# Gate and up products for two steps at once in 64x32 tiles, with fewer PSUM banks for outputs and features

## The reference

```python
x = x + _layernorm(attn(_layernorm(x), Wq, Wk, Wv, Wo))
# feed-forward, 512 -> 2048 -> 512, weights from cubic interpolation of control points
gate = einsum('bsh,ih->bsi', layernorm(x), gate_w)
up = einsum('bsh,ih->bsi', layernorm(x), up_w)
inter = silu(gate) * up
x = x + _layernorm(einsum('bsi,hi->bsh', inter, down_w))
```

## Time and profile before

| | us |
|---|---|
| median of 3 runs | 821.23 (818.14 to 821.86) |
| profiled execution | 818.13 |
| its span | 816.3 |
| first gate matmul of the feed-forward block | 413.4 |
| PE busy in the span | 742.2 (91%) |
| DVE, ACT, POOL busy | 530.1, 370.3, 445.9 |

### The profile page before, as it was taken

One profiled execution on the slowest core, in us unless ns is written; L12 is line 12 of the kernel. 1 busy time (PEld: TensorE's weight loads), 2 busy tenths in 40 slices (PEclk: granted clock), 3 DMA queues, 4 the chain that ended last, 5 costly groups with the idle time before them and its releaser, 6 DMA issues. The chain is left out here.

```text
span 816.3 us, 19133 instructions
## 1 busy us (share of the span) xinstructions
PE 742.2 (91%) x7152; PEld 506.3 (62%) x7152; DVE 530.1 (65%) x1025; ACT 370.3 (45%) x633; POOL 445.9 (55%) x616
## 2 busy tenths in 40 slices
PE   5887799999999999799857899999989999999996
PEld 3665577877687768677533466566656556565565
DVE  6752964587546863465656677878777787775453
ACT  2420332333232323232346666666656665666541
POOL 5289948556763759601425455455455555456542
PEclk9897799999999999989989999999999999999999
DMA  8614647333661448501881515545353553535313
GB/s 286 218 52 123 200 148 242 98 116 123 200 195 35 158 154 269 137 3 48 257 298 36 193 46 184 157 150 175 120 180 106 168 170 130 169 100 185 119 53 104
DMA packets 64313, 120.54 MB, mean 148 GB/s; under 512 B 12144, under 2 KB 28656, under 8 KB 62192
## 3 DMA queue, kind: packets, MB, share of 16 engines
q1 hardware_dynamic: 64240, 119.53, 45.2%
HBM read 82.94 MB, written 36.57 MB: 146 GB/s over the span
## 5 line engine op out<-in xcount | busy, mean ns | idle before, releaser
L1240 POOL TENSOR_TENSOR act<-inter,act 128x512 f16<-128x512 f32 x128 | 158.4, 1248 | 126.8 <-ACT act L1281 126.8
L1354 DVE SCALAR_TENSOR_TENSOR inter<-ubank,c_up,gated 128x512 f32<-128x512 f32 x128 | 95.9, 749 | 74.9 <-ACT gated L1285 74.2
L1494 PE MATMUL ybank<-down,act 128*128 128x160 f16 x512 | 110.5, 235 | 0.0
L1495 PE MATMUL ybank<-down,act 128*128 128x160 f16 x512 | 109.5, 233 | 0.0
L1496 PE MATMUL ybank<-down,act 128*128 128x160 f16 x512 | 109.5, 233 | 0.0
L1285 ACT ACTIVATE gated<-gbank,c_gate 128x512 f32<-128x512 f32 x128 | 87.9, 686 | 44.6 <-PE gbank L1453 44.6
L1281 ACT CAST act<-inter 128x512 f16<-128x512 f32 x128 | 79.1, 618 | 48.6 <-DVE inter L1354 48.5
L1494 PEld LDWEIGHTS ybank<-down,act 128*128 128x128 f16 x512 | 50.1, 98 | 39.2 <-issue 35.5
L1453 PE MATMUL gbank<-z,s_twice 128*32 128x512 f16 x512 | 51.8, 394 | 9.0 <-PEq L84 3.5
L728 PE MATMUL ybank<-ga_hi,xT_hi 128*128 128x512 f32 x128 | 51.8, 405 | 6.1 <-ACT shared L520 4.7
L520 ACT ACTIVATE shared<-ybank,yr 128x512 f32<-128x512 f32 x32 | 22.0, 689 | 71.9 <-POOL yr L363 71.9
(11 more groups left out here) (191 smaller groups left out, 2078.5 us busy)
## 6 DMA issues: line engine op xcount, KB each, us to landing
x_ln<-x SPq DMA_DIRECT2D x64, 256.0 KB, 3.3
z<-token_features SPq DMA_DIRECT2D x16, 1024.0 KB, 5.5
job<-job_in SPq DMA_DIRECT2D x24, 640.0 KB, 4.4
shared<-x SPq DMA_DIRECT2D x32, 256.0 KB, 2.7
x<-shared SPq DMA_DIRECT2D x32, 256.0 KB, 2.0
token_features<-z_hi SPq DMA_DIRECT2D x64, 128.0 KB
token_features<-z_lo SPq DMA_DIRECT2D x64, 128.0 KB
x_res<-x SPq DMA_DIRECT2D x32, 256.0 KB, 2.9
```

Of the source, the lines that this page charges most:

```text
L1240: pool.tensor_tensor(hidden[par][:, i, TOK:2 * TOK], inter[:, i % INTERS, :], hidden[par][:, i, 0:TOK], ALU.subtract).then_inc(inter_ready, 1)
L1354: dve.scalar_tensor_tensor(out=inter[:, i % INTERS, :], in0=ubank[:], scalar=c_up[:], in1=gated[:, i % 2, :], op0=ALU.mult, op1=ALU.mult). ...
L1494: pe.matmul(out, hidden[par][:, r, high], box[:, 0], start=False, stop=False)
L1495: pe.matmul(out, hidden[par][:, r, high], box[:, 1], start=False, stop=False)
```

## The change

**Gate and up.** `gate_up` is called once for two steps, i and i + 1. Its matmuls use 64 of the 128 rows and 32 columns, so that eight tiles fill the array: four column tiles times two row halves. For z, the two row halves now hold different tiles of the token features, with high and low values in different rows of the buffer (`u // 2 * 2 + low`). The products are high times high, high times low, low times high: three passes of eight matmuls for gate and three for up, for two steps, where there were eight passes of four. A step's eight halves go so that the two row halves of one column tile write to banks of different steps. Four banks hold gate and up of the two steps. A `sem_inc` on PE carries the wait for the banks.

**Banks.** The output banks become one (`outbank`), emptied by ACT for even q and by DVE for odd q; the last group uses gate and up banks beside it. The feature banks become one (`zbank`): `products` runs its half 0 in the second half of a quad and its half 1 in the first half of the next quad, after DVE has emptied half 0 (`z_half_ready`); the transpose of the next tile waits until half 1 is emptied.

**Order.** ACT, DVE and POOL do silu, product and rounding for pairs of steps. `load_z` is two DMAs of 64 partitions. The DRAM tensor has high and low beside each other.

```diff
-                    pe.wait_ge(z_loaded[par][i // HALF], count * 16)
-                side, c = i // HALF, i % HALF
-                for w, bank, free, done in ((GATE, gbank, silu_done, gate_done), (UP, ubank, inter_done, up_done)):
-                    if not (isinstance(n, int) and n == 0):
+                    pe.wait_ge(z_loaded[par][i // HALF], count * 32)
+                side, first = i // HALF, isinstance(n, int) and n == 0
+                for w, banks, free, done in ((GATE, gbanks, silu_done, gate_done), (UP, ubanks, inter_done, up_done)):
+                    if not first:
                         pe.wait_ge(free, n)
-                    for part, start in ((s_twice, True), (s_low, False)):
+                        pe.sem_inc(banks_free, 1)
+                    for part, low, start, stop in ((s_twice, 0, True, False), (s_twice, 1, False, False),
+                                                   (s_low, 0, False, True)):
                         for u in range(4):
-                            rows = slice(32 * u, 32 * u + 32)
-                            mm = pe.matmul(bank[rows], part[:, side, c, w, rows], z[par][:, i // 4 * 4 + u, :],
-                                           start=start, stop=not start)
-                    mm.then_inc(done, 1)
+                            for e in range(2):
+                                rows, at = slice(64 * (u % 2), 64 * (u % 2) + 64), 32 * (u ^ e)
+                                mm = pe.matmul(banks[e][at:at + 32],
+                                               part[rows, side, (i + e) % HALF, w, 32 * u:32 * u + 32],
+                                               z[par][rows, i // 4 * 4 + u // 2 * 2 + low, :], start=start, stop=stop)
+                    mm.then_inc(done, 2)
...
-        gbank, ubank, tbank, zbank = [psum(n, [P, BANK], F32) for n in ("gbank", "ubank", "turned", "zbank")]
-        ybank = [psum(f"ybank{q}", [P, BANK], F32) for q in range(2)]
+        gbanks = [psum(f"gbank{e}", [P, BANK], F32) for e in range(2)]
+        ubanks = [psum(f"ubank{e}", [P, BANK], F32) for e in range(2)]
+        zbank, ybank = [psum(n, [P, BANK], F32) for n in ("zbank", "outbank")]
...
-            def quad(g, par, count, j, made, begun, more):
+            def quad(g, par, count, j, made, begun, more, owed):
                 m = g * Q + j + AHEAD
                 first = isinstance(g, int) and g == 0
-                for s in range(4):
-                    i = 4 * j + s
+                for i in (4 * j, 4 * j + 2):
                     n = g * I + i
                     if i + 2 < I:
                         gate_up(n + 2, i + 2, par, count)
                     elif not (isinstance(n, int) and n >= STEPS - 2):
-                        gate_up(n + 2, i + 2 - I, 1 - par, count + par)
+                        gate_up(n + 2, 0, 1 - par, count + par)
+                    if i == 4 * j and owed:
+                        feats.products(pe, m - 1, z_banks, (1,))
                     if i == 0 and not first:
                         moment_pair(g - 1, I // 2 - 1, 1 - par)
-                    elif i % 2 == 0 and i:
+                    elif i:
                         moment_pair(g, i // 2 - 1, par)
                     if not first:
                         part(g - 1, i, 1 - par)
-                    if s == 1 and made:
+                    if i == 4 * j + 2 and made:
+                        feats.products(pe, m, z_banks, (0,))
+                    if not first:
+                        part(g - 1, i + 1, 1 - par)
+                    if i == 4 * j and made:
                         feats.turn(pe, m, z_banks, id16)
-                    if s == 2 and made:
-                        feats.products(pe, m, z_banks)
...
         sp.wait_ge(feats.z_spilled[half], (g + 1) * feats.SPILLS // 2 * 16)
-        sp.dma_start(z[:, half * self.half:(half + 1) * self.half, :],
-                     feats.spilled[half].rearrange("a k f t n -> (a k f) t n")).then_inc(self.z_loaded[par][half], 16)
+        pairs = self.half // 2
+        for two in range(2):
+            sp.dma_start(z[64 * two:64 * two + 64, half * self.half:(half + 1) * self.half, :],
+                         feats.spilled[half][:, :, two * pairs:(two + 1) * pairs].rearrange("k f t a n -> (k f) (t a) n")
+                         ).then_inc(self.z_loaded[par][half], 16)
```

More of the change, by code:

```diff
@@ L977, in turn_copy, with z_low @@
         dve.tensor_copy(self.hT[:].rearrange("p a k n -> p (a k n)"), banks[1].bitcast(F16)).then_inc(self.hT_copied, 1)
-    def z_low(self, dve, m, q, banks, buf=0):
+    def z_low(self, dve, m, q, banks, buf=0, halves=(0, 1)):
         K = self.K
         high, low_t = self.z_parts[buf]
-        for half in range(2):
+        for half in halves:
             dve.wait_ge(self.z_hi_done, m * 2 + half + 1)
@@ L1000, in turn, with products @@
         mm.then_inc(self.hT_done, 1)
-    def products(self, pe, m, banks):
+    def products(self, pe, m, banks, halves=(0, 1)):
         feat, hT = self.feat, self.hT
-        pe.wait_ge(self.hT_copied, m + 1)
-        for half in range(2):
+        for half in halves:
+            if half == 0:
+                pe.wait_ge(self.hT_copied, m + 1)
+            elif halves == (1,):
+                pe.wait_ge(self.z_half_ready, m + 1)
             cols = slice(half * self.ZCOLS, (half + 1) * self.ZCOLS)
@@ L1268, in _ @@
             low(0, 0, 0)
+            low(1, 1, 0)
             feats.scale(pool, Q + 2)
@@ new lines, in product_pair, with quad @@
+            def product_pair(g, i):
+                for e in range(2):
+                    product(g * I + (i + 2 + e), i + 2 + e)
+            def quad(g, par, count, j, made, begun, more, owed):
+                i, m = 4 * j, g * Q + j + AHEAD
+                loads = g + (1 + (j + AHEAD + 1) // RING)
+                for before, q in outputs(g, i, 0):
+                    if q % 2 == 1:
+                        y_out(before, q)
+                if made:
+                    feats.norm(dve, m, (j + AHEAD) % RING)
+                product_pair(g, i)
+                if owed:
+                    feats.z_low(dve, m - 1, (j + 1) % Q, z_banks, 1 - par if j == 3 else par, (1,))
+                if made:
+                    feats.low(dve, m)
+                if begun:
+                    feats.stats(dve, m + 1, (j + AHEAD + 1) % RING, loads)
+                for before, q in outputs(g, i, 0):
+                    o_stats(before, q)
+                if i == 0 and not (isinstance(g, int) and g == 0):
+                    moment_lo(g - 1, 1)
+                if made:
+                    feats.turn_copy(dve, m, z_banks)
+                if not (isinstance(g, int) and g == GROUPS - 1 and j == Q - 1):
+                    product_pair(g, i + 2)
+                if made:
+                    feats.z_low(dve, m, (j + 2) % Q, z_banks, par if j < 2 else 1 - par, (0,))
+                for before, q in outputs(g, i + 2, 2):
+                    o_finish(before, q)
+                if j == Q - 1:
+                    moment_lo(g, 0)
@@ L1766, in feature_tables @@
     assert (high.astype(np.float64) + low == feat).all()
-    features = np.stack([high, low], 1).reshape(P, 2, K, T * FEATURES)
+    halves = [t.reshape(P, K, 2, T // 4, 2, FEATURES).swapaxes(3, 4) for t in (high, low)]
+    features = np.stack(halves, 1).reshape(P, 2, K, T * FEATURES)
     return features, points.reshape(K * FEATURES, 5, -1), coef.reshape(K * FEATURES, 5, -1).astype(np.float32)
```

176 lines of the change are left out of this document (85 added, 91 removed).

## The result

The changed kernel takes **852.09 us** (median of 4 runs, 847.2 to 854.26), the one before 821.55 beside it (4 runs, 818.14 to 825.64): a ratio of 1.035, with an interval of 1.030 to 1.040. The change is slower by 3.5%. The forecast of 823 us and its range of 808 to 840 are both missed. "Slower" was the direction with the highest chance, 0.42. Of that, 0.20 was the upper part of case A, at most 831 us; the rest was put at 834 and at 857, each for a reason that isn't the one found.

A forecast was written before the change was run, and what follows sets the result against it. PE was taken as the bound, with the z refill next to no slack behind it; group terms summed to +1.2 us, with 0.3 us waits +2: 820 profiled, 823 us as median, range 808 to 840.

The forecast's parts named there:

- case A: The forecast itself: the z refill sets each group's length, three quarters of PE's gain turns idle; 815 to 831 us, chance 0.60.
- 857: Rival in gate/up: the two row halves take turns, 24 passes for 12, a group 53.5 us; 857 us, chance 0.10.
- PE's work: PE's quads: eight tiles run in the time of four, 0.96 us less a quad, 30.7 us less over 32 quads.
- The refill becomes the bound: Each group's first gate: PE idles some 4.3 us for the z load; the way around takes 47.4 us.
- The second z load: Refill on SP: z load as two DMAs adds a second issue of 0.34 us, 0.3 more; landing kept at 5.4.
- The clock: PE around first gates: idle time lowers the clock, costing 1.3 us a group, between 0 and 1.7.
- The loop's return: Groups 2 to 5: the stall of 2.1 us at 608 us stays, some 2.5 with its clock.
- Groups 1 and 6: From each one's first gate to the next group's: +0.4 us for group 1, +1.4 for group 6, before waits of 0.3 each.
- Group 0: First group: pairs make the chain of silu and products faster, then the refill's fixed 14 us follow; -1.0 us.
- Rival E: DVE: `o_finish` at a quad's end delays `h_lo` more than laid out, 1.5 us more a group; 834 us, chance 0.12.
- The start of the block: Stretch up to group 0's first gate: the sum has no term for it.
- Behind group 7's gate: After group 7's first gate, no refill: 3.5 quads gain 3.7 us, the clock gives back 1.3; -2.4 us.

The follow-up runs named there:

- b_twoload: Kernel before the change, with each half of z loaded by two DMAs of 64 partitions instead of one of 128: 837.42 us.
- a_warm: Changed kernel, with 22 matmuls whose sums nobody reads ahead of each wait for z, to keep PE busy: 844.83 us.
- a_early2: Changed kernel, SP spilling and loading z earlier, the output's store ahead of the z load, q = 0's high part waiting only for its own half's spill: 808.31 us.
- e2_norm: `a_early2` with DVE's norm of the next token block moved ahead of `z_low` of half 0: 804.45 us.
- b_norefill: Kernel before the change, without the refill of z (features spilled and loaded once, for group 0): 818.66 us.
- before: The kernel without the change: 821.55 us.
- after: The kernel with the change as made: 852.09 us.
- a_early: Changed kernel, SP spilling half 0 in quad 1 and loading it at once, ahead of the output's store; half 1 spilled at quad 2's start: 828.38 us.

## Why the prediction was wrong

By its own steps, for the profiled execution (820 forecast, 854.3 measured):

- **PE's work: right.** Eight tiles make a pass of 0.22 us, and a full group without refill gains 4.3 us against 3.8. PE's busy sum falls by the forecast 31 us between the kernels without refill; with it by only 14 (742 to 728), as matmuls at half clock count for longer.
- **The refill becomes the bound: right**, as the mechanism of case A, which had 0.60. The way around is also as laid out up to the spill: from the first gate to `o_finish` 29.2 to 30.3 us against 28.7 (in groups 2, 3, 5 and 6; the loop's return is in group 4), and from there to the first spill 3.7 to 7.5, in the mean 5.5 as forecast.
- **The second z load: mis-sized.** The sum gives it the 0.34 us of a second issue, which is SP's cost, and leaves the landing at 5.4. Measured are 7.1 to the last landing. From first spill to gate there are 16.4 to 16.8 us for the 14.8 of the sum, so 1.6 to 2.0 more in each of groups 1 to 6; with 1.3 in group 0 that is some 12 us. In the kernel before the same split costs 15.5 us in all (`b_twoload`). This is the largest wrong term, and I never bounded it from above.
- **The clock: mis-sized.** 1.3 us a group, bounded by 1.7 with one low stretch of 3.4 us. The low stretches were 3.4 to 10.2 us long, and from the gate to `o_finish`, where groups 2, 3, 5 and 6 took 29.2 to 30.3 us, all four take 27.6 or 27.7 with the clock kept up (`a_warm`): 1.6 to 2.7 us a group.
- **The loop's return: mis-sized.** The sum kept 2.5 us, the 2.1 of before with its clock. The idle time was 6.1 us, and group 4's way to `o_finish` is 7 to 8 us longer than that of the groups beside it. That is some 5 us more than the sum has. Written out, groups 2 to 5 are 11.4 us shorter in the profile, the whole kernel 7.1 in the medians. Why the gap grew stays open.
- Together these three make groups 2 to 5 217.3 us instead of 198.5: some 7 from the landing, 5 from the clock and 5 from the loop's return; what is left lies between `o_finish` and first spill, which took 7.3 and 7.4 us in two of the four groups for the 5.5 of the sum. Groups 1 and 6 are 49.0 and 50.5 instead of 47.0 each.
- **Group 0: wrong sign.** -1.0 forecast, +7.2 measured. I argued that pairs shorten the chain of silu and products and left DVE's durations at those of the earlier trace rows. Two of them more than double beside back-to-back pairs on GpSimd, PE then idles 3.4 us before the transposes in three quads, where before it was 1.2, and the mean clock over the group is 0.73 of full (0.93 before). Of the 52.5 us, 2.9 go with SP's new order (49.6 in `a_early2`) and 4.3 more with the norm's new place (45.3 in `e2_norm`). Rival E had DVE late, but by `o_finish`; in its place `o_finish` got shorter (0.75 us on average instead of 1.36).
- **The start of the block:** +1.9 us, forecast as unchanged; an idle stretch of 5.6 us, for 3.5 before, that the profile puts down to PE's sequencer. It differs by as much between kernels whose code is the same there (5.4 us in `b_norefill`, 4.6 to 8.0 in the others), and I leave it open.
- **Behind group 7's gate:** -2.4 forecast, -2.2 measured.

The range failed because its upper end was built from rivals one at a time. The terms of A itself had bounds too narrow: the landing (0.3, real 2) and the clock (1.7, real up to 2.7) lie on the same path in group after group, and the loop's return (2.5, real 7 to 8) once on that path. DVE beside GpSimd (nothing, real some 4) lengthened group 0.

## What to carry to other kernels

When an engine on the bound gets faster, find the next path around the loop that has no slack, and move that first. The same change is 3.5% slower with SP's old order and 1.7% faster with a new one. On such a path every small term counts once per turn, so bound each from above: what lands last, not what it costs to issue; idle time with the half-clock stretch that follows it. Beside back-to-back work on GpSimd two of DVE's ops took more than twice as long here, so durations may not be taken from a trace in which the engines ran in another order.

## What the runs showed of the hardware

- Eight matmuls of 64x32 tiles, two row halves into each bank but into different 32-partition groups, start as one pass of 0.22 us.
- Two DMAs of 64 partitions (512 KB each) issued together land 4.8 and 6.6 us behind their own issues, 7.1 in all, where one of 128 partitions takes 5.4. One DMA whose outermost dimension is 2 takes over 22 us for the same 1 MB.
- PE's clock was 1.2 GHz from 565.4 to 575.6 us, around the end of an idle stretch of 7.7 us (562.2 to 569.9), and stayed at 2.4 GHz where matmuls without use filled the same wait.
- PE stood 2.1 to 6.1 us where a loop over groups returned (`before`, `after`), and not there where the loop was written out.
- A DVE norm from SBUF to SBUF took 0.54 us alone and 1.38 when it started just behind an op of GpSimd, and an op with two SBUF inputs (`h_lo`) 1.62 so, and 0.68 when it started first.
- With a store of 256 KB issued behind a z load of 1 MB on one queue, the loads of `x_ln`, which leave after the wait for that store, left 17.3 us after the first spill (546.01 to 563.27 in `a_early`); with the store ahead of the load 11.6 (538.85 to 550.43 in `a_early2`).
